# Flamingo block on one core: the LayerNorm's second tile moves from VectorE to GpSimd

## What is computed

```
x = x + tanh(g_xattn[0]) * cross_attention(ctx, layernorm(x))      # 8 heads, masked
x = x + tanh(g_ffn[0])   * routed_self_attention(layernorm(x))     # 4 of 16 heads, chosen per batch
x = x + tanh(g_xattn[1]) * depool(layernorm(x), ctx)
x = x + tanh(g_ffn[1])   * expert_layer(layernorm(x))              # 2 of 8 experts, and a shared one

layernorm(x) = (x - mean(x)) / sqrt(var(x) + 1e-5)                 # over the 128 features
```

## Time and profile before

| what | us |
|---|---|
| median of 3 runs | 220.06 |
| lowest, highest | 219.15, 224.03 |
| profiled execution, its own time | 221.45 |
| span of the profiled execution, first to last instruction | 219.2 |
| mean granted TensorE clock, share of full | 0.974 |

### The profile page before, as it was taken

One profiled execution on the slowest core, in us unless ns is written; L12 is line 12 of the kernel. 1 busy time (PEld: TensorE's weight loads), 2 busy tenths in 40 slices (PEclk: granted clock), 3 DMA queues, 4 the chain that ended last, 5 costly groups with the idle time before them and its releaser, 6 DMA issues.

```text
span 219.2 us, 4482 instructions
## 1 busy us (share of the span) xinstructions
PE 200.2 (91%) x1515; PEld 157.6 (72%) x1515; DVE 131.0 (60%) x400; ACT 112.2 (51%) x300; POOL 84.7 (39%) x146
## 2 busy tenths in 40 slices
PE   0989999999999799898998999999989999998994
PEld 0968786767786788556675686877768868886884
DVE  3487876743494455759564476568558456656331
ACT  0065063154653523874355589762779655483640
POOL 5402620104038535306154443655408416521460
PEclk9999999999999857999999999999999999999998
DMA  5995000002001100200002100002000000000001
GB/s 184 344 385 246 4 0 27 0 28 73 3 0 42 31 3 24 74 3 0 0 27 56 45 0 0 3 1 55 21 0 14 14 0 0 1 10 17 0 1 51
DMA packets 8152, 9.81 MB, mean 45 GB/s; under 512 B 895, under 2 KB 7360, under 8 KB 8002
## 3 DMA queue, kind: packets, MB, share of 16 engines
q10 hardware_dynamic: 3470, 5.88, 7.5%
q1 hardware_dynamic: 4020, 2.32, 3.8%
q0 software_dynamic: 640, 1.32, 2.2%
HBM read 8.47 MB, written 1.05 MB: 43 GB/s over the span
## 4 chain that ended last, share of the span: by engine, by line
PE 70%; DVE 10%; ACT 8%; ACTq 5%; issue 5%; POOL 2%; POOLq 0%; DVEq 0%
PE act_bank L668 6%; PE act_bank L669 6%; PE dve_bank L674 6%; PE dve_bank L511 4%; PE act_bank L527 4%; PE act_bank L580 3%; PE act_bank L614 3%; PE dve_bank L435 3%; PE act_bank L538 3%; DVE mx L984 3%; PE act_bank L594 2%; PE dve_bank L695 2%; PE dve_bank L658 2%; PE act_bank L585 2%; PE dve_bank L623 2%
## 5 line engine op out<-in xcount | busy, mean ns | idle before, releaser
L1179 POOL TENSOR_TENSOR ctok<-ctok,cT 128x256 f32<-128x256 f32 x28 | 20.4, 730 | 26.0 <-DVE cT L1072 22.1
L760 ACT ACTIVATE pT<-act_bank 128x512 f32<-128x512 f32 x32 | 16.5, 602 | 24.8 <-PE act_bank L527 24.8
L836 ACT ACTIVATE hx<-act_bank,we 128x256 f32<-128x256 f32 x32 | 15.2, 475 | 18.4 <-PE act_bank L669 18.1
L984 DVE TENSOR_REDUCE mx<-dve_bank 128x2 f32<-128x512 f32 x32 | 19.9, 684 | 7.6 <-PE dve_bank L511 7.6
L1167 POOL TENSOR_SCALAR p<-p,rec 128x256 f32<-128x256 f32 x32 | 14.7, 477 | 24.7 <-DVE rec L1023 24.7
L1072 DVE SCALAR_TENSOR_TENSOR cT<-dve_bank,we,hx 128x256 f32<-128x256 f32 x32 | 14.8, 478 | 10.6 <-PE dve_bank L674 9.6
L668 PE MATMUL act_bank<-xw,we 128*128 128x256 f32 x64 | 19.3, 383 | 1.6 <-DVE xw L1065 0.9
L669 PE MATMUL act_bank<-xw,we 128*128 128x256 f32 x64 | 19.0, 379 | 0.0
L674 PE MATMUL dve_bank<-hx,we 128*128 128x256 f32 x64 | 18.3, 388 | 0.1
L809 ACT ACTIVATE p<-act_bank,nm 128x256 f32<-128x256 f32 x32 | 14.7, 485 | 4.2 <-DVE nm L1019 4.1
L837 ACT ACTIVATE hx<-act_bank,we 128x256 f32<-128x256 f32 x32 | 15.0, 468 | 0.0
(11 more groups left out here) (190 smaller groups left out, 461.1 us busy)
## 6 DMA issues: line engine op xcount, KB each, us to landing
we<-pack_e ACTq DMA_DIRECT2D x1, 1936.0 KB, 11.6
ctok<-ctx_tokens ACTq DMA_DIRECT2D x1, 1024.0 KB, 10.2
w2h<-head_weights SPq DMA_DIRECT2D x8, 97.5 KB, 2.0
cT<-ctx_features ACTq DMA_DIRECT2D x3, 256.0 KB, 7.6
wb<-pack_b ACTq DMA_DIRECT2D x1, 594.5 KB, 7.9
wa<-pack_a ACTq DMA_DIRECT2D x1, 582.0 KB, 4.6
depool_rows<-dp SPq DMA_DIRECT2D x4, 128.0 KB, 1.8
out_tokens<-xs SPq DMA_DIRECT2D x4, 128.0 KB, 2.3
```

The costliest lines, as they stand in the source:

```text
L760: act.activation(pT1[:, h].rearrange("p c t -> p (c t)"), abank(n + j)[:], ACT.Exp, scale=HD1 ** -0.5).then_inc(act_done, 1)
L836: act.activation(hx[:, k % EXPERT_BUFS, 0, :], bank[:, 0:T], ACT.Silu, bias=X("b1")[:, i:i + 1])
L984: dve.tensor_reduce(mx[:, b % 2, i, :, 32 * j + ROW_MAX], dbank(n + j)[:].rearrange("p (t s) -> p t s", t=TT), AX.X, ALU.max).then_inc(dve ...
L1179: ins = pool.tensor_tensor(yT[:, b % 2, :], yT[:, b % 2, :], prod[:, k % EXPERT_BUFS, :], ALU.add)
```

## The change

At a `norm` step VectorE now normalises tile 0 alone and raises `xn_done`. GpSimd gets a `norm` step of its own, at the place in its order that is in brackets above: it waits for its own `rstd_done` and for the same buffer, normalises tile 1 and raises the new semaphore `xn_odd_done`. TensorE waits for `xn_done` ahead of the first transpose and for `xn_odd_done` ahead of the second.

```diff
@@ tensor engine, step "norm"
                     bank = take_act(na)
                     for t in range(TT):
+                        if t == 1:
+                            pe.wait_ge(xn_odd_done, NORM_AT[step] + 1)
                         mm = pe.transpose(bank[:, t * P:(t + 1) * P], xn[:, NORM_AT[step] % XN_BUFS, t, :], ident)
                     mm.then_inc(act_full, 1)
@@ vector engine, step "norm"
-                    for t in range(TT):
-                        ins = dve.tensor_scalar(xn[:, k % XN_BUFS, t, :], x_of(i, b)[:, t, :],
-                                                mv[:, b, i, t, 0:1], rstd[:, b, i, t:t + 1],
-                                                ALU.subtract, ALU.mult)
-                    ins.then_inc(xn_done, 1)
+                    dve.tensor_scalar(xn[:, k % XN_BUFS, 0, :], x_of(i, b)[:, 0, :], mv[:, b, i, 0, 0:1],
+                                      rstd[:, b, i, 0:1], ALU.subtract, ALU.mult).then_inc(xn_done, 1)
@@ gpsimd
+                elif what == "norm":
+                    k = NORM_AT[step]
+                    pool.wait_ge(rstd_done, STAT_AT[("stat", b, i)] + 1)
+                    if k >= XN_BUFS:
+                        pool.wait_ge(act_full, ACT_AT[NORMS[k - XN_BUFS]] + 1)
+                    pool.tensor_scalar(xn[:, k % XN_BUFS, 1, :], x_of(i, b)[:, 1, :], mv[:, b, i, 1, 0:1],
+                                       rstd[:, b, i, 1:2], ALU.subtract, ALU.mult).then_inc(xn_odd_done, 1)
```

More of the change, by code:

```diff
@@ L311, in flamingo @@
         rstd_done = sem("rstd_done")
-        xn_done = sem("xn_done")
+        xn_done, xn_odd_done = sem("xn_done"), sem("xn_odd_done")
         v1_done = sem("v1_done")
```

## The result

| | us |
|---|---|
| before, median of 4 runs | 220.05 (219.15 to 224.03) |
| after, median of 4 runs | 231.44 (228.08 to 232.58) |
| ratio | 1.043 (95% interval 1.029 to 1.057) |
| profiled execution after: its own time, span, clock | 228.08, 225.9, 0.962 |

It is slower, as forecast, but by 11.4 us in the medians where I gave 4.0. Medians are of all executions; the ratios leave out those more than 1.5% above the fastest of the same kernel. The profiled execution is the fastest of its four, 6.6 us above the profiled one of before (221.45), which lies above its own median.

What follows compares the result with a forecast made beforehand. TensorE, working in list order, bounds the kernel. Four late places, 1.35 + 0.75 + 0.3 + 1.4 = 3.8 us, less 0.1 relief plus 0.3 for later GpSimd steps, made +4.0: 224.1 us from 220.06, range 221.3 to 227.2.

Steps and rivals of the forecast that it cites:

- VectorE's relief: VectorE drops one tensor_scalar per norm, 4.2 us of work in all; perhaps 0.1 us comes back, at `norm:1.3`.
- the rival of the other side: Pairs ready sooner where TensorE waits for VectorE's tiles: 1.0 us at one place, 0.2 at two, total 218.7 us; chance 0.05.
- The four places: GpSimd's tile late at `norm:1.1`, `norm:2.1`, `norm:3.1`, `norm:3.2` and neighbours: +1.35, +0.75, +0.3, +1.4 us.
- the covered ones: Seven norms, both at the start, `norm:2.0`, `0.1`, `0.3`, `1.3`, `2.3`, where GpSimd is ready in time: cost 0, at most 0.1.
- The absorbed case: Rival: TensorE's later idle time takes up half of the 3.8 us of stalls, giving 221.8 us; chance 0.18.
- the cost of one tile: GpSimd's new 128x128 tensor_scalar taken as 0.37 us, 16 times, 5.9 us in all.
- The prediction's own sign for this: In the profile after, the forecast counts as wrong if GpSimd's tile takes over 0.5 us.
- The bound: Upper limit for GpSimd's tile: a 128x256 tensor_tensor takes 730 ns, and half the columns can't take more.
- the first place: `norm:1.1`, `norm:3.0`, `norm:0.2`, where GpSimd's tiles come behind `gather:2.0`: +1.35 us, bounds 1.2 and 2.4.
- the clock: Rival: the first stall puts off TensorE's rise from half clock, 2.4 us on top, 226.5 us; chance 0.23.
- The argument against the clock: In 102 to 104 us TensorE was busy 1.10 of 2 us and kept full clock, so a stall needn't lower it.
- The 0.15 us for tiles hindering each other: VectorE's and GpSimd's tiles of a pair, partly overlapping, ready 0.6 us after the root: +0.15 or -0.2 us where it comes last.

Runs made afterwards that it cites:

- e9: Against the kernel before, tile 1 is not normalised at all and TensorE transposes tile 0 twice: 218.93 us against 219.22, ratio 0.998.
- e7: Against the kernel before, VectorE still does both tiles but signals each, and TensorE waits for each: 218.95 us against 219.49, ratio 1.000.
- e11: Against the kernel before, only the six norms where TensorE came late anyway have GpSimd's odd tile: 219.48 us against 219.22, ratio 1.000.
- e6: Changed kernel with identity transposes filling TensorE's waits at four norms: 227.55 us, against 230.31 for the unfilled changed kernel.
- e5: Changed kernel unaltered, on another chip with more executions: 230.31 us against 219.49 for the kernel before, ratio 1.056.
- e3: Changed kernel with GpSimd's tile moved right behind its root in GpSimd's list, same arithmetic: 225.54 us, ratio 1.033 to the kernel before.
- e1: Changed kernel with four forms of GpSimd's tile by norm number: 794 and 718 ns with subtraction, 366 and 461 without.
- e2: Changed kernel with GpSimd's tile multiplying by root and 1, no subtraction, at all 16 norms: 224.84 us against 219.37 before, ratio 1.024.
- e8: Changed kernel with three adding forms and one subtracting second, by norm number: 437 and 440 ns adding with two scalars, 808 subtracting.
- e12: Changed kernel with GpSimd's tile right behind its root and a negated mean added instead of subtracted: 222.12 us against 219.22 before, ratio 1.010.

## Why the prediction was wrong

**What bounds the kernel: right.** TensorE's order did. VectorE's relief, 0.1 us in the sum, is at most small: e9's ratio is 0.998, and in its trace 0.8 us come back at `norm:3.1` and `norm:2.2`. That is most of the 1.0 which the rival of the other side had for this place; its 0.2 at two others can't be made out. But that is with an odd tile that costs nothing, and the rival's condition, GpSimd's steps being over before TensorE comes, wasn't met: the adds ended at 149.73, behind TensorE's first transpose. Its 218.7 is out by the result. The wait itself costs nothing measurable (e7).

**The four places: right.** The order in GpSimd's list made the stalls, at the places named and from the steps named, and the covered ones cost nothing (e11). None of the stalls was absorbed later: the table shows each shift kept to the end. The absorbed case is out. (Its figure was also off in itself: half of 3.8 is 1.9, and with the forecast's 0.2 for the rest it would have been 222.2 and not 221.8.)

**The step that failed first: the cost of one tile.** "I take 0.37 us, the row of the same shape and kind" was mis-sized; it measured 0.80. The kind was not the same: the rows of before have GpSimd multiply, and this one subtracts. The prediction's own sign for this, a tile of over 0.5 us, was there. The bound failed as well, 0.73 us "can't take more than that", since the add in that row isn't a subtraction either. With 0.80 in the forecast's own sums: 1.35 + 3 x 0.43 = 2.6 for the first place, 0.75 + 0.43 = 1.2, 0.3 + 2 x 0.43 = 1.2 and 1.4 + 0.43 = 1.8. That is 6.8 us, and 7.0 with the 0.2 for the rest. The places measured 3.0, 1.1, 1.1 and 2.0 in the profiled execution, 7.2 in all.

**The second: the clock stood among the rivals and belonged in the sum.** The 7.0 us have no term for it, and the medians lie 11 us apart. I gave it 0.23 and 2.4 us on top; filling the waits gave back 2.8 us net of what the filler costs (e6). That the pair of profiled executions fits a sum without the clock is partly luck, in two ways. First, before was itself at half clock there, from within 74 to 75 until within 84 to 85. e7, as fast as the kernel before, was at half only from 76.4 to 79.8 and takes 35.2 us to `route:1.0` and 30.3 to `route:2.0`. Against these the changed kernel in e5, on the same chip, loses 4.7 and 5.5 us, where the sum with 0.80 has 2.6 and 1.2. Second, the half clock from 84.8 to 90.6 in the changed kernel cost nothing further on: between `route:1.0` and the first transpose of `norm:2.1` TensorE was busy 27.5 us in place of 26.3, but the stretch took 29.4 against 29.3, so its idle time took that up. In e5 it was busy 31.5 us and the stretch took 33.4. The argument against the clock, that TensorE at 102 to 104 idled 0.9 us and kept its clock, was read from a shorter idle time in a busier stretch. At the first place TensorE idled 2.3 us of 4, and beside it lay the half-clock stretch of before. How long a wait brings the half clock back, and for how long, isn't shown by these runs.

**The ports.** The 0.15 us for tiles hindering each other was near: beside VectorE's, GpSimd's tile took 0.86 us (e3) against 0.80. It is a small part of the cause at most. At 112.3 in e3 VectorE's tile took 0.35 us with GpSimd's beginning 0.07 behind it. So two short tensor_scalars ran side by side, where a VectorE one beside the long add took up to 895 ns. The rule of a full block, cited above from the Trainium skill, "SBUF — State Buffer", section "Who interferes with whom", is stronger than what is seen here for the short pair.

## What to carry to other kernels

An operation moved to another engine must be priced by a row with the same arithmetic operation on that engine: on GpSimd a subtraction took 0.80 us where add or multiply took 0.44, and negating the mean once avoids it. An engine that works in a fixed order starts a moved piece when the steps ahead of it are over, so read its list and not its busy share (39%) before giving it something that TensorE waits for. Where TensorE is kept at full clock with filler, a new wait of 2 us can cost more than its length, and filler inside the wait gets some of it back.

## What the runs showed of the hardware

- GpSimd's tensor_scalar on 128x128 float32, means of groups: 361 to 408 ns with one scalar from memory, 437 to 509 with two, 718 to 853 with a subtraction in either position (e1, e2, e8, e12). VectorE's with a subtraction: 345.
- A stall of 2.3 us, with a shorter one behind it, was followed by 13.6 us at 1.2 GHz, from 84.2 to 97.8, through nearly unbroken work (e5).
- The executions of one kernel scatter with the clock: among the 29 of before beside e9 to e12, the median is 217.9 us for the six with a mean clock of 0.992 and 219.2 for the eleven with 0.984, and the two with 0.967 took 222.0 and 222.6.
